# A patch-embedding, attention and mixture-of-experts kernel on one core: one block in place of two, token routing regrouped, and sixteen unread products on TensorE

## What is computed

```
h = concat([tokenize(x), txt], axis=1)                      # 64 x 69 x 256
h = h + attention(_layernorm(h), wq, wk, wv)                # 16 heads of 16
h = h + moe(_layernorm(h), router, w13, w2)
# moe: the two largest of 8 router logits, softmax of the two as weights;
# tokens sorted by expert; per expert: silu(x @ gate) * (x @ up) @ w2, hidden width 512;
# each row times its weight, added back to its token
```

## Time and profile before

| | us |
|---|---|
| median of three runs (lowest, highest) | 798.04 (793.64, 799.46) |
| the profiled execution, its own time | 790.39 |
| span of the profiled execution, first to last instruction | 788.5 |
| of the span: front up to the last sequence's values (step 66) | about 399 |
| of the span: end of the front and routing, to the first gate product | 399 to 453.85 |
| of the span: expert tiles | 453.85 to 788.5 |

### The profile page before, as it was taken

How to read it: one execution, slowest core, us unless ns; L and a number is a source line. 1 busy time by engine, 2 the same in 40 slices (tenths; PEclk the granted TensorE clock), 3 DMA queues, 4 the chain that set the end, 5 groups by cost and what they waited for, 6 DMA issues and landing times. The chain is left out here.

```text
span 788.5 us, 27483 instructions
## 1 busy us (share of the span) xinstructions
PE 688.5 (87%) x9624; PEld 476.1 (60%) x9624; DVE 544.4 (69%) x1163; ACT 420.6 (53%) x951; POOL 437.0 (55%) x602
## 2 busy tenths in 40 slices
PE   5858999999899999988961389999999999999992
PEld 4625667677677777766750246666666666666661
DVE  5968988888888887887677745565555655556551
ACT  1234666688778877787735334444434444343430
POOL 6662554565766666553443126666666666666652
PEclk9967999999999999999855589999999999999996
DMA  8687576554555555544411038778877888778772
GB/s 289 199 245 232 164 245 193 157 158 148 153 169 166 151 153 177 153 130 145 124 42 11 21 67 131 130 126 132 130 127 134 129 130 131 128 132 131 130 116 39
DMA packets 145129, 111.70 MB, mean 142 GB/s; under 512 B 93433, under 2 KB 125961, under 8 KB 144936
## 3 DMA queue, kind: packets, MB, share of 16 engines
q1 hardware_dynamic: 129911, 86.74, 43.0%
q0 software_dynamic: 15088, 23.21, 17.0%
HBM read 58.95 MB, written 24.10 MB: 105 GB/s over the span
## 5 line engine op out<-in xcount | busy, mean ns | idle before, releaser
L1296 POOL DMA_INDIRECT out<-y,token_of x76 | 120.5, 1586 | 102.3 <-DVE own L1373 85.3
L1345 DVE SCALAR_TENSOR_TENSOR hid<-quad,up_scale,silu 128x512 f32<-128x512 f32 x76 | 57.1, 751 | 104.5 <-PE quad L1387 104.5
L1387 PE MATMUL quad<-w_hi,x_hi 128*128 x304 | 116.2, 382 | 3.4 <-DVE x_lo L1352 2.3
L1387 PE MATMUL quad<-w_lo,x_hi 128*128 x304 | 116.2, 382 | 0.0
L1387 PE MATMUL quad<-w_hi,x_lo 128*128 x304 | 116.0, 382 | 0.0
L1387 PE MATMUL bank<-w_hi,hidT 128*128 x608 | 113.2, 274 | 2.6 <-DMA hidT<-hid_parts 2.6
L1320 ACT ACTIVATE silu<-quad,unscale 128x512 f32<-128x512 f32 x76 | 52.3, 688 | 107.8 <-PE quad L1387 107.8
L653 DVE TENSOR_REDUCE nm_src<-quad 69x16 f32<-69x1104 f32 x64 | 83.0, 1296 | 30.9 <-PE quad L1056 30.7
L920 ACT ACTIVATE probs<-quad 69x1104 f32<-69x1104 f32 x64 | 69.6, 1088 | 44.9 <-PE quad L1139 44.9
L1282 POOL DMA_INDIRECT wc<-xn_rows,token_of x73 | 73.0, 1000 | 37.0 <-issue 21.3
L1387 PE MATMUL bank<-w_lo,hidT 128*128 x304 | 83.5, 275 | 0.0
(11 more groups left out here) (226 smaller groups left out, 1722.9 us busy)
## 6 DMA issues: line engine op xcount, KB each, us to landing
w_lo<-in_experts_w SPq DMA_DIRECT2D x24, 512.0 KB, 6.0
w_raw<-in_experts_w SPq DMA_DIRECT2D x48, 256.0 KB, 5.0
xt<-in_patches SPq DMA_DIRECT2D x18, 384.0 KB, 5.6
h<-h_rows SPq DMA_DIRECT2D x34, 128.0 KB, 5.6
hb<-h_rows SPq DMA_DIRECT2D x34, 128.0 KB, 5.3
out<-h SPq DMA_DIRECT2D x34, 128.0 KB, 4.6
xn_rows<-xn SPq DMA_DIRECT2D x34, 128.0 KB, 4.8
vb<-v SPq DMA_DIRECT2D x30, 138.0 KB
```

The source lines that it names most:

```text
L1296: nc.gpsimd.indirect_dma_start(out, bass.IndirectOffsetOnAxis(token_of[:, n:n + 1], 0), y[q][:, :], None, compute_op=ALU.add).then_inc(add ...
L1345: nc.vector.scalar_tensor_tensor(out=hid[q][:, :], in0=quad[:, 2 * q + 1, :], scalar=up_scale[:, :], in1=silu[q][:, :], op0=ALU.mult, op1= ...
L1387: last = nc.tensor.matmul(dst, x[:, k, :], w[:, bass.ds(col + k * (2 * width if width == HIDDEN else width), width)], start=(k == 0 and m ...
```

## The change

1. **One block.** `experts()` is gone; its five streams are called at the end of the streams of `front()`, on tiles that the front no longer uses (the names change: `x_hi` is now `fx_hi`, `hid` is `oT`, `silu` is `xT`, `hidT` is `xt`, `hid_parts` is `kE` and `kO`, `y` is `hb`). No barrier stands between.
2. **Routing earlier and in groups.** `CHOOSE`, `COUNTED`, `RANK` stand one step earlier. The count over groups uses sums over blocks of five groups (`in_group`), so 11 products instead of 31 for the first 30 groups. The marks of twelve pieces are spread over steps 67 to 71, two in each, and two behind.
3. **Two operands in PSUM.** `lanes` and `places` (0, 1, 2, ... along the row) are copied into a bank of `quad` once, and the marks read them from there.
4. **The tables.** `passed` (L725 to L729 of the new kernel) and `is_expert` (L725 to L743) are made on POOL, by three and five operations of 128x608; `passed` ahead of the first gathers, `is_expert` behind their issue. DVE keeps the sum over `passed` and the copy to `expert_of`, now ahead of its wait for the last placing product. The weight of tile 0 waits for the finished table.
5. **Sixteen products** 128x512 (`WARM`) on PE behind the last placing product, into PSUM that nobody reads, ahead of its wait for `token_of`.
6. Small: several semaphores of a chain are merged into one counter per engine.

```diff
-                CHOOSE, COUNTED, RANK = BATCH, BATCH + 1, BATCH + 3
-                LANES = {BATCH + 4 + k: range(3 * k, 3 * k + 3) for k in range(4)}
+                CHOOSE, COUNTED, RANK = BATCH - 1, BATCH, BATCH + 2
+                LANES = {BATCH + 3 + k: range(2 * k, 2 * k + 2) for k in range(5)}
...
+                            if t == min(LANES):
+                                dve.wait_ge(s["probs_ready"], BATCH)
+                                then(nc.vector.tensor_copy(lanes_ps, lanes))
+                                then(nc.vector.tensor_copy(places_ps, places))
...
-                            nc.vector.tensor_tensor(at_lane[n], lanes[:, None, :].broadcast_to([P, GROUP, P]), lane_f[:, j, b, None].broadcast_to([P, GROUP, P]),
+                            nc.vector.tensor_tensor(at_lane[n], lanes_ps[:, None, :].broadcast_to([P, GROUP, P]), lane_f[:, j, b, None].broadcast_to([P, GROUP, P]),
...
-                            for m in range(lo, min(hi, G - 1)):
-                                behind = G - 1 - m
-                                to = nc.tensor.matmul(b4[:, (m + 1) * EXPERTS:G * EXPERTS].rearrange("p (g e) -> p g e", e=EXPERTS), ones_h,
-                                                      both[:, m, None, :].broadcast_to([P, behind, EXPERTS]), start=False, stop=(m == G - 2), skip_group_check=True)
+                            for m in range(GROUP - 1):
+                                to = nc.tensor.matmul(ranks[:, from_:to_, m + 1:, :], ones_h,
+                                                      both_groups[:, from_:to_, m, None, :].broadcast_to([P, to_ - from_, GROUP - 1 - m, EXPERTS]),
+                                                      start=False, stop=(to_ == GROUPS and m == GROUP - 2), skip_group_check=True)
+                            for b in range(from_, min(to_, GROUPS - 1)):
+                                at = (b + 1) * GROUP
+                                to = nc.tensor.matmul(b4[:, at * EXPERTS:G * EXPERTS].rearrange("p (g e) -> p g e", e=EXPERTS), ones_h,
+                                                      in_group[:, b, None, :].broadcast_to([P, G - at, EXPERTS]), start=False, stop=False, skip_group_check=True)
...
+                        def edge_steps(to, edge, count):
+                            nc.gpsimd.tensor_tensor(to, places[:, :, None].broadcast_to(TE), edge[:, None, :].broadcast_to(TE), ALU.subtract).then_inc(s["table_parts"], 1)
+                            pool.wait_ge(s["table_parts"], count + 1)
+                            nc.gpsimd.tensor_scalar(to, to, 1.0, 0.0, ALU.add, ALU.max).then_inc(s["table_parts"], 1)
+                            pool.wait_ge(s["table_parts"], count + 2)
+                            nc.gpsimd.tensor_scalar(to, to, 1.0, None, ALU.min).then_inc(s["table_parts"], 1)
+
+                        edge_steps(passed, tile_end, 2)
...
                         for n in range(DEPTH):
                             nc.gpsimd.indirect_dma_start(xg[n], None, xn_rows, bass.IndirectOffsetOnAxis(token_of[:, n:n + 1], 0)).then_inc(gathered[n], 16)
+                        edge_steps(is_expert[:, :, :], first_tile, 5)
+                        pool.wait_ge(s["table_parts"], 8)
+                        nc.gpsimd.tensor_tensor(is_expert[:, :, :], is_expert[:, :, :], passed, ALU.subtract).then_inc(s["table_parts"], 1)
+                        pool.wait_ge(s["table_parts"], 9)
+                        nc.gpsimd.tensor_scalar(is_expert[:, :, :], is_expert[:, :, :], y_scale[:, :], None, ALU.mult).then_inc(s["table_parts"], 1)
+                        experts_pool(pool)
...
+                        dve.wait_ge(s["table_parts"], 5)
+                        then(nc.vector.tensor_reduce(expert_f, passed, AX.X, ALU.add))
+                        then(nc.vector.tensor_copy(expert_of[:, :], expert_f))
                         dve.wait_ge(s["placed"], PLACED)
...
+                            if n == 0:
+                                dve.wait_ge(s["table_parts"], 10)
+                            nc.vector.tensor_tensor(own_row, xg[n % DEPTH][:, DIM:], is_expert[:, n, :],
+                                                    ALU.mult).then_inc(d["own_ready"], 1)
...
+                        pe.wait_ge(s["w_hi_ready"], CHUNKS)
+                        for k in range(WARM):
+                            nc.tensor.matmul(quad[:, 1 + k % 2, :], ones_h, w_hi[:, 0:BANK], start=True, stop=True)
+                        pe.wait_ge(s["tokens_ready"], 1)
+                        experts_pe(pe)
```

430 lines of the change are left out of this document (215 added, 215 removed).

## The result

The changed kernel takes 794.20 us in the median of 20 executions (788.27 to 799.28), beside 798.75 us (793.36 to 805.95) for the kernel before in the same comparison: a ratio of 0.9949, 95% interval 0.9926 to 0.9972. It is faster, by about half of the 8 us that were forecast (790.0, range 784 to 796). In the later comparisons eight executions of the kernel before and one of a version lie over 1.5% above the fastest of their kernel and are left out of the ratios.

The account below looks back on a forecast made before the run. PE bounds the tile stage; before it one DVE-led chain sets the time. Tile 1 starting 9.8 us earlier, less 1.9 for the clock, gives 7.9: 790.4 becomes 782.5 in the profile, median 790, range 784 to 796.

Parts of the forecast that it names:

- Count of places: PE's place count before the last attention division: products take 1.4 us instead of 4.11, the division starts 1.8 us earlier.
- Marks: DVE from that division to the last choice: PSUM operands free POOL, so the choice starts 7.5 us earlier.
- Rival 3: Beside DVE's marks: PSUM doesn't free POOL, choice 4.2 us later, first table 2 us late, 796 us; chance 0.05.
- From the choice to the list: Last choice to first gather: 0.8 us for DVE held by POOL's table plus 0.4; gather 6.3 us earlier.
- Barrier and tile 0: Barrier gone, PE begins when the gather lands, 3.1 us after issue; unread products hidden, tile 0 at full clock.
- The table on POOL: Between gathers and tile 1: five POOL operations take 6.7 us and delay tile 1, which starts 9.8 us earlier than before.
- Rival 4: POOL's wide table operations: at 3 us average each no gain, over 4.6 each 806 us or more; chance 0.05.
- The clock: PE's standstill before tile 1 loses the full clock again, costing tile 1 1.9 us.
- Sum: At the head of the tile stage: 9.8 less 1.9 gives 7.9 us earlier, new median 790.
- Rival 1: Before tile 1: clock holds through the wait, or the table is cheap; 787 to 788 us; chance 0.18.
- Rival 2: The front gives less: value products held or last logits late, choice 3 to 4 us later, 793 to 795; chance 0.20.
- Rival 5: Before tile 0: the sixteen products don't raise the clock, yet the sum stays; its chance is part of Rival 1's.

Follow-up runs that it names:

- marks_read_sbuf: The changed kernel, but DVE's marks and tile matrices read lane and place numbers from SBUF again, not PSUM: 803.26 us, ratio 1.0033 to the kernel before.
- before_psum: The kernel before with only lane and place numbers copied into PSUM and read there by marks and tile matrices: ratio 0.9950, repeated 0.9971.
- the barrier's run: The changed kernel with the expert table made by two DVE operations and the barrier between routing and tiles put back: ratio 0.9888 to the kernel before.
- after_fill: The changed kernel with 24 unread products instead of 16 ahead of the first rows, and 24 more between tiles 0 and 1: ratio 0.9898 to the kernel before.
- table_on_dve: The changed kernel with the expert table made by two operations on DVE instead of on POOL: 787.38 us, ratio 0.9860 to the kernel before.

## Why the prediction was right or wrong

The direction, most of the mechanisms and the range held. The size didn't: 4.1 us (0.5%, by the ratio; 4.6 between the medians) in place of 8. The step that failed is the price of the table on POOL, 6.7 us forecast and 8.9 measured. By the prediction's own steps, on the scale of the first profile, with the last maximum as its fixed point:

**Count of places: size a little high.** 1.5 us of products as forecast (1.4). I let 1.8 us reach the path; undoing it costs 1.2, without the earlier steps that my 1.8 included.

**Marks: right.** The choice starts 8.2 us earlier (29.38 against 37.62); I took 7.5. No POOL operation takes over 2 us beside the marks. `marks_read_sbuf` and `before_psum` show that this rests wholly on the PSUM operand. Rival 3 named what the copies prevent, at three quarters of the price: 4.2 and 2 us, where the undoing cost 6.9 and 1.06. Its second part had it the wrong way round, since the first table wasn't held and DVE's matrices were.

**From the choice to the list: 0.5 us short.** 23.36 us against 21.63, 1.7 more in place of my 1.2. What I gave 0.8 for is there with 0.6: DVE's L1026 takes 0.81 us beside POOL's table, and took 0.23 before. Another 1.0 I had put at nothing: DVE waits 1.23 us for ACT's exponential (L1195, 0.25 before). I counted the eight sets that ACT numbers behind it, and not the three that now stand between the steps and the exponential and keep ACT busy until 422.9. Together the first gather comes 6.5 us earlier; forecast 6.3.

**Barrier and tile 0: half right.** What I took for the barrier's wait, DVE's last operation, was most likely POOL's third issue (see the barrier's run); the landing of the gather, on which the sum rests, was right. PE turned the first rows 3.0 us behind the gather's issue (3.1). The clock was full by 440, as I had it; but tile 0 didn't run at it. I asked whether the products end in time and not what the 2.2 us between them and the rows do. I had even read a stop that ended in a fall of the clock, and used it only for the second standstill. (I read it as 2.2 us; a mean clock of 0.78 over that microsecond puts the fall at 772.6, 2.0 us behind the stop.) It cost nothing here, since the table came later still.

**The table on POOL: the step that failed.** I took 6.7 us, with 9.2 as the upper bound; it took 8.9 (445.68 to 454.56). The two-input operations were cheaper than my rate, 1.26 and 1.48 us against 1.74 each. The three with one input, for which I chose 0.9 near the memset's rate, took 2.27, 1.75 and 1.82. The choice "since they read and write once" was wrong: the nearest rows were a memset, which reads nothing, and an addition, and in these rows each one-input `TENSOR_SCALAR` costs more than either operation with two inputs; the one with two steps is the dearest. Why is not shown. By the upper bound of 1.74 each I would have been at 9.2 and the sum at 5.4 us, nearer than what I gave. Rival 4's price (3 us on average) wasn't reached, 1.7 was.

The Trainium skill, GPSIMD Engine Reference, section 3.1 Elementwise, gives 1.03 cycles per element for a loop of at most two operations and about 1.8 as the best case of another, an estimated 0.5 and 0.9 us for 608 columns at 1.2 GHz, and here 1.75 to 2.27 us were measured; for two inputs its 2.6 cycles, an estimated 1.3 us, agree with 1.26 and 1.48.

**The clock: right.** 1.9 us for tile 1; 2.0 measured here (4.76 us), 1.6 and 1.7 in the two repetitions (4.38 and 4.45), and `after_fill` gives them back.

**Sum.** 9.8 became 8.3 us at tile 1 (67.01 against 75.34), less 2.0: 6.3 us at tile 2, where I had 7.9. The table's 2.2 us too much, less 0.6 by which the three gathers were issued faster than I took (3.64 us) and 0.2 in the front, are that difference but for rounding. The 0.75 us behind PE's last product, the 0.15 outside the span and an open rest are what lies between the 6.3 to 6.9 us of the profiles and the 4.1 to 4.6 of the comparisons. The assumption under the sum, "a shift at the head of that stage reaches the end of the program undiminished", held only to about 1 us, since the program ends with POOL's stores and not with PE.

**The rivals.** Rival 1 (clock holds, or table cheap) didn't happen, but is what `after_fill` and `table_on_dve` make of the kernel. Rival 2 (the front gives less) didn't happen as I put it: the logits were in time, though only just (saved 0.05 us behind the end of the marks). Rival 5 is right in its conclusion: without the products the time is the same.

**A better version.** The table made by DVE with 24 products beats both kernels: 0.9842, 0.9892 and 0.9860 in three comparisons, some 11 us less than the kernel before.

## What to carry to other kernels

When a wait is removed, price the one that comes next as carefully as the one that goes: here 5.7 us of what the barrier freed went to a table that had been moved off DVE, where it would have cost 1.4 us in a gap. Unread products are to be sized by their end, not by their start: here those that ended 0.4 to 1.6 us ahead of the next real product left it the full clock, those that ended 2.2 us ahead or more didn't, and in one profile 24 ended too late and held PE up by 0.6 us. And an edit that frees an engine is worth what the other end of the same wait allows: 3.7 us alone, 8.0 us together with the rest.

## What the runs showed of the hardware that I had not expected

- On POOL an operation of 128x608 with one input (1.75 to 2.27 us, 2.9 to 3.7 ns per column) is dearer than one with two (1.23 to 1.48 us, 2.0 to 2.4 ns); on DVE the same table took 0.78 + 0.54 us.
- A standstill of PE of 2.2 us behind products at the full clock was enough for tile 0 to run mostly at half, though the clock fell only when PE was busy again: 1.00 in 443 to 444, 0.68 in 446 to 448, 0.50 in 448 to 450. In the second standstill it fell while PE was idle (0.89 in 452 to 454, PE done by 451.3). Standstills of 0.41 to 1.63 us behind products at the full clock cost at most 0.1 us in tile 0 in six profiles.
- DVE's matrices with both inputs in SBUF took 7.60 us beside POOL's wide table and 6.54 with one in PSUM, and POOL's operation 2.27 us both times: there DVE paid. A small operation of POOL beside eight dense ones of DVE with both inputs in SBUF was held for 6.01 us.
- PE's first instruction behind the barrier between two blocks came 3.60 to 3.68 us behind the end of POOL's last gather issue in all five profiles that have the barrier.
- The execution's time exceeded the span of its instructions by 1.86, 2.00 and 2.36 us on average for three kernels.
- The front of 64 steps moves by up to 11.5 us between executions of one kernel, and most of that arises in its first sixteen steps (the sixteenth maximum lies at 136.35, 142.55 and 145.09 us in the three profiles of the version with 24 products, the last at 388.10, 395.10 and 399.61).
